# Batches 0 and 1 of the second norm, their transposes and their routing scores move into attention 2's last slots and drain; the scores move to another bank

## The reference

```python
x = x + layernorm(attention_1(layernorm(x)))          # 16 heads of 16, causal
x = x + layernorm(ffn(layernorm(x)))

# ffn(hidden):
h = rmsnorm(hidden, ln1_w)
q, k, v = h @ Wq, h @ Wk, h @ Wv                      # 32 query heads, 4 key/value heads, 128 wide
q, k = rope(q), rope(k)
o = softmax(causal(q @ k.T / sqrt(128))) @ v @ Wo     # attention 2
x = hidden + o
t = rmsnorm(x, ln2_w)
scores = sigmoid(t @ Wr)                              # 32 experts
idx = top_k(scores + expert_bias, 8)
w = scores[idx] / sum(scores[idx])
moe = sum over e of w_e * (silu(t @ Wg_e) * (t @ Wu_e)) @ Wd_e
return x + moe + silu(t @ Wsg) * (t @ Wsu) @ Wsd      # plus the shared expert
```

## Time and profile before

| | |
|---|---|
| median of 3 executions | 948.99 us (947.24 to 949.40) |
| the profiled execution | 950.87 us, of which the span from first to last instruction is 948.80 us |
| granted clock of PE, mean | 0.970 of full speed |
| PE busy | 867.5 us, 91% |
| DVE, ACT, POOL busy | 616.5 us (65%), 570.5 us (60%), 455.9 us (48%) |
| attention 2, slots 56 to 70 | from about 574 us to 651.3 us |
| block of the experts | from 651.76 us on |

### The profile page before, as it was taken

How to read it: one execution, slowest core, us unless ns; L and a number is a source line. 1 busy time by engine, 2 the same in 40 slices (tenths; PEclk the granted TensorE clock), 3 DMA queues, 4 the chain that set the end, 5 groups by cost and what they waited for, 6 DMA issues and landing times. The chain is left out here.

```text
span 948.8 us, 18792 instructions
## 1 busy us (share of the span) xinstructions
PE 867.5 (91%) x6108; PEld 802.1 (85%) x6108; DVE 616.5 (65%) x1620; ACT 570.5 (60%) x1570; POOL 455.9 (48%) x486
## 2 busy tenths in 40 slices
PE   5799998767999999999999999978999999999994
PEld 4699897657999998999899999867888888888884
DVE  5456667647787787778777777755444544544546
ACT  6788888656766766667666667654333333433333
POOL 3743334357867766777776777720222222221221
PEclk9799999978999999999999999997999999999998
DMA  7001000131114111421111111200433333333321
GB/s 234 1 1 46 22 23 1 59 93 39 35 46 142 38 45 35 114 66 46 34 46 35 46 45 36 51 1 18 144 116 116 114 98 115 101 114 116 112 82 45
DMA packets 50246, 63.34 MB, mean 67 GB/s; under 512 B 5728, under 2 KB 36064, under 8 KB 50176
## 3 DMA queue, kind: packets, MB, share of 16 engines
q1 hardware_dynamic: 49088, 61.41, 22.2%
q10 hardware_dynamic: 1088, 1.05, 0.3%
HBM read 41.86 MB, written 1.18 MB: 45 GB/s over the span
## 5 line engine op out<-in xcount | busy, mean ns | idle before, releaser
L639 POOL TENSOR_TENSOR b_prob<-b_prob,b_rsum 128x256 f32<-128x256 f32 (+1 forms) x128 | 104.7, 839 | 108.3 <-DVE b_rsum L621 108.3
L73 PE MATMUL banks<-act_t,b_w 128*128 128x256 f32 (+1 forms) x392 | 129.3, 330 | 3.9 <-DVE b_work L1194 2.8
L74 PE MATMUL banks<-act_t,b_w 128*128 128x256 f32 (+1 forms) x392 | 127.2, 324 | 0.0
L75 PE MATMUL banks<-act_t,b_w 128*128 128x256 f32 (+1 forms) x392 | 127.0, 324 | 0.0
L1955 ACT ACTIVATE moe_hid<-banks 128x512 fp32r<-128x512 f32 x66 | 39.5, 598 | 124.1 <-DVE banks L2046 124.1
L1355 ACT ACTIVATE b_prob<-banks,b_negmax 128x128 f32<-128x128 f32 (+1 forms) x256 | 103.6, 416 | 13.3 <-DVE b_negmax L1342 12.9
L2039 DVE TENSOR_TENSOR moe_gated<-banks,moe_share 128x512 f32<-128x512 f32 x66 | 45.6, 691 | 85.0 <-PE banks L75 80.9
L1211 ACT ACTIVATE b_qt<-b_work 128x512 fp32r<-128x512 f32 x64 | 40.5, 632 | 97.5 <-POOL b_work L1206 97.5
L639 POOL TENSOR_TENSOR a_prob<-a_prob,a_rsum 128x256 f32<-128x256 f32 x64 | 52.0, 834 | 82.2 <-DVE a_rsum L621 82.2
L1206 POOL TENSOR_TENSOR b_work<-b_work 128x512 f32<-128x512 f32 x64 | 86.7, 1355 | 9.2
L1202 POOL TENSOR_TENSOR b_work<-b_work,rope_t 128x512 f32<-128x512 f32 x64 | 84.2, 1315 | 8.2 <-DMA b_work<-b_work 8.2
(11 more groups left out here) (237 smaller groups left out, 3026.0 us busy)
## 6 DMA issues: line engine op xcount, KB each, us to landing
b_work<-b_work SPq DMA_DIRECT2D x128, 128.0 KB, 2.3
moe_share<-gates SPq DMA_DIRECT2D x32, 512.0 KB, 3.6
b_w_raw<-in_b_wq SPq DMA_DIRECT2D x4, 1024.0 KB, 5.5
b_w_raw<-in_b_wo SPq DMA_DIRECT2D x4, 1024.0 KB, 9.6
a_src_t<-act_t SPq DMA_DIRECT2D x5, 512.0 KB, 2.9
moe_w_raw<-in_wg SPq DMA_DIRECT2D x16, 128.0 KB, 2.2
moe_w_raw<-in_wu SPq DMA_DIRECT2D x16, 128.0 KB, 2.3
moe_w_raw<-in_wd SPq DMA_DIRECT2D x16, 128.0 KB, 2.3
```

Of the source, the lines that this page charges most:

```text
L73: nc.tensor.matmul(out, w_lo, m_hi, start=start, stop=False, skip_group_check=skip)
L74: nc.tensor.matmul(out, w_hi, m_lo, start=False, stop=False, skip_group_check=skip)
L75: return nc.tensor.matmul(out, w_hi, m_hi, start=False, stop=stop, skip_group_check=skip)
L639: last = self.m.nc.gpsimd.tensor_tensor(rows, rows, rsum[:, :, t:t + 1].to_broadcast([PART, 2, width]), ALU.mult)
```

## The change

The plans of PE, ACT and DVE in attention 2 are rewritten. Moments of batches 0 and 1 move from slot 64 to slots 56 and 60; their roots from slot 65 to slot 61, among the exps of slots 61, 62 and 63; their factors from 66 to 62; their rows from 67 to 63 and 64; their transposes from 68 to 63 and 64; their routing from 68 and 69 to 66 and 67. Batch 2's moments stay in slot 65, its roots go from 65 to 66, its rows stay in 67, its transposes in 68, its routing goes from 70 to 69. Batch 3's transposes go from slot 69 to 70. The banks of the transposes are permuted, so that batches 0 and 1 use the banks 4 and 5 that attention 2 frees first, and the routing scores go from bank 3, which holds transposed probabilities, to bank 4. Waits for the freed tiles are added. In the experts PE no longer waits for the sigmoid, since the sigmoid now reads another bank than the second gate product writes.

```diff
-        self.turn2 = Turn(m, ctx, "h2", rows, m.act_t, banks=(0, 1, 4, 5), weight=m.lnw[:, 1, :])
+        self.turn2 = Turn(m, ctx, "h2", rows, m.act_t, banks=(4, 5, 0, 1), weight=m.lnw[:, 1, :])
...
             def turn_h2(b):
-                pe.wait_ge(*{0: (self.exp_done, 2 * self.STAGES),
-                             1: (self.exp_done, 2 * self.STAGES),
-                             2: (self.kt_ready, self.ITS),
-                             3: (self.raw_ready, self.STAGES)}[b])
+                if b == 0:
+                    pe.wait_ge(self.kt_ready, self.ITS)
+                elif b == 1:
+                    pe.wait_ge(self.raw_ready, self.STAGES)
+                    pe.wait_ge(self.cos_ready, self.STAGES)
+                else:
+                    pe.wait_ge(self.exp_done, 2 * self.STAGES)
                 self.turn2.tensor(pe, b)
 
             def route(b):
-                pe.wait_ge(self.pt_ready, self.STAGES)
                 pe.wait_ge(self.turn2.lo_done, b + 1)
                 router_scores(m, b)
...
-                4: ((turn_h2, 0), (turn_h2, 1), (turn_h2, 2), (route, 0)),
-                5: ((turn_h2, 3), (route, 1)), 6: ((route, 2),)})
+                -1: ((turn_h2, 0),), 0: ((turn_h2, 1),), 2: ((route, 0),), 3: ((route, 1),),
+                4: ((turn_h2, 2),), 5: ((route, 2),), 6: ((turn_h2, 3),)})
...
             def rows(b):
+
+                if b == 0:
+                    for swapped in self.swapped:
+                        act.wait_ge(swapped, self.SWAPPED * (self.STAGES // 2))
+                elif b == 2:
+                    act.wait_ge(self.q_added, self.STAGES)
...
-                1: ((roots, 0), (roots, 1), (roots, 2), (expert_0, 0)),
-                3: ((rows, 0), (rows, 1), (rows, 2)),
-                4: ((turn, 0), (turn, 1), (roots, 3)), 5: ((rows, 3), (turn, 2)), 6: ((turn, 3),)})
+                -3: ((roots, 0), (roots, 1)), -1: ((rows, 0),), 0: ((rows, 1), (turn, 0)),
+                1: ((turn, 1), (expert_0, 0)), 2: ((roots, 2),), 3: ((rows, 2),), 4: ((turn, 2), (roots, 3)),
+                5: ((rows, 3),), 6: ((turn, 3),)})
...
-                0: ((moments, 0), (moments, 1)), 1: ((moments, 2),),
-                2: ((factors, 0), (factors, 1), (factors, 2)), 4: ((moments, 3), (turn, 0)),
-                5: ((factors, 3), (turn, 1)), 6: ((turn, 2), (turn, 3))})
+                -8: ((moments, 0),), -4: ((moments, 1),), -2: ((factors, 0), (factors, 1)), 0: ((turn, 0),),
+                1: ((turn, 1), (moments, 2)), 2: ((factors, 2),), 4: ((moments, 3), (turn, 2)),
+                5: ((factors, 3),), 6: ((turn, 3),)})
...
-        out = m.banks[:, 3, (NTT * b + t) * NE:(NTT * b + t + 1) * NE]
+        out = m.banks[:, 4, (NTT * b + t) * NE:(NTT * b + t + 1) * NE]
...
             pe_up(pe, 0, 0, 0)
-            pe.wait_ge(sigmoid_done, 1)
...
-            nc.scalar.activation(score[:].rearrange("p t e -> p (t e)"), gu[1][1][:, 0:NT * NE],
+            nc.scalar.activation(score[:].rearrange("p t e -> p (t e)"), m.banks[:, 4, 0:NT * NE],
```

## The result

| | median | range | runs |
|---|---|---|---|
| before | 947.79 us | 945.25 to 951.51 | 20 |
| changed | 950.91 us | 948.03 to 953.41 | 20 |

The ratio is 1.0031, 95% interval 1.0021 to 1.0040: slower by 2 to 4 us (3.1 between the medians), against 0.9 forecast. The profiled execution took 950.99 us (span 949.1).

A forecast was written before the change was run, and what follows sets the result against it. PE bounds the kernel, so the change acts only where PE waits, from slot 57 until the expert loop is full. +3.7 in front and -2.8 in the tail give +0.9: 949.9 us; 8-in-10 range 946.9 to 952.6.

The forecast's parts named there:

- slower: Outcome in which the time lies more than 0.2%, 1.9 us, above the kernel before; chance 0.27.
- What would show it: Signs listed: later marks in slots 60, 61; wait 2.7 us before slot 63; last projection 642.2; block 651.5 to 652.9.
- (a): Slot 57: batch 0's moments before the maximum delay POOL's chain; PE's slot 60 starts +0.86 us later, ends 0 to 1.28.
- (b): Slot 61: batch 1's moments before the maximum delay the reciprocal POOL waits for, with no slack: +1.28 us.
- (c): Slots 61 and 62: the roots' Sqrt load is hidden, but the Exp reload delays slot 62's exp: +1.28 us.
- (d): Drain, slots 63 on: factors and rows delay projection 59 by +0.8 us; the drain gives back 0.5.
- a rival: Slower by the clock: half clock in slot 63 after a longer wait, up to 1.5 us on projection 59; chance 0.28.
- (e): Tail behind the last projection: 2.8 us shorter at half clock, 4.0 at full clock; half clock was taken.
- The rival's total: Slower by the clock, with half clock in slot 63: together +2.4 us, 951.4; chance 0.28.
- (f): Things said to cost nothing: scores' bank, removed sigmoid wait, added waits, shared expert's weights; no DMA added or moved.
- the last part of the rival: First expert products: the clock rises later, gates find PE late, up to 1 us more, 952.3; chance 0.28.
- the intended gain: Rival: nothing in front is delayed, the tail's 2.8 to 4.0 us are gained, 945.0 to 946.2; chance 0.04.

The follow-up runs named there:

- the first two experiments: Kernel before with moments of batches 0 and 1 in slots 56 and 60: 951.18 us; the same with their roots in slot 61: 954.46 us.
- roots early: Kernel before with moments of batches 0 and 1 in slots 56 and 60 and their roots in slot 61: 954.46 us, ratio 1.0058.
- The fastest kernel: Changed kernel with moments of batches 0 and 1 before DVE's outputs of slots 62 and 63, their roots in slot 64, among other moves: 944.25 us, ratio 0.9958.

## Why the prediction was right in its range and wrong in its middle

The mechanism stood as forecast: a delay in front, a shorter tail, a difference small against both. The range held the time and the forecast of 949.9 was 1.0 us off, but the difference of 2 to 4 us is "slower" by the 1.9 us that I had set as the border, and I had given that 0.27. Part of the nearness is luck: I built on the 948.99 us of three executions, and over 20 the kernel before has 947.79. The difference, 3.1 us at the medians and 2.15 anchored, was missed by 2.2 and 1.25. The marks of "What would show it" that are times of the axis flatter the forecast in the same way: the last projection at 642.74 and the block at 652.15 lie near or within what I gave (642.2; 651.5 to 652.9), but this execution reached the anchor 1.82 us earlier than that of before. The sum by its steps, anchored:

| step | forecast | measured |
|---|---|---|
| (a) moments of batch 0 | +0.86 | +1.33 |
| (b) moments of batch 1 | +1.28 | +1.42 |
| (c) reload of the exp table | +1.28 | +1.42 (1.40 between the first two experiments, 1.37 without the loads) |
| (d) slot 63, clock kept | +0.8 | +0.96 |
| (d) rest of the drain | -0.5 | -0.2 |
| clock in slot 63 | 0 (a rival: +1.5) | +1.1 to +1.2 |
| (e) tail | -2.8 | -3.91 |
| first expert products | 0 | -0.06 |
| sum | +0.9 | +2.15 |

**(a) was mis-sized by how I used a wait.** I let POOL's 0.91 us in slot 58 absorb part of the 1.28. The wait shrank by 0.20, and POOL still started 1.32 late there, after 1.43 in slot 57. The wait names the reciprocal, which follows VectorE's query, ScalarE's query, and POOL's rotation of the slot before. In the changed kernel each of them waits for the next:

```profile
588.14 0.63 ACT L1211 ACTIVATE b_qt<-b_work 128x512 fp32r<-128x512 f32 x1 [2.58 <-POOL b_work L1206]
588.80 0.86 DVE L1216 TENSOR_TENSOR b_qt<-b_work,b_qt 128x512 fp32r<-128x512 f32 x1 [1.07 <-ACT b_qt L1211]
```

POOL was waiting for its own work to come round. The keys' transposes did come 0.86 later, as forecast (16.51 against 15.65), but the scores behind them waited for a split of the keys that ScalarE issues behind the exps, and those were a full 1.3 late. (b) and (c) went as written, 0.14 over each, which is mostly overlap lost: the first instruction of the moments begins 0.71 behind the addition where the maximum began 0.60 behind it, and the load of the table begins when the query has ended (614.78), where in the kernel before the exp began 0.09 ahead of the query's end.

**The clock in slot 63 is the step that failed.** Of two like cases in the profile of before, one with a fall and one without, I took none. I put the fall at nothing. It fell in both traces of the changed kernel and cost 1.1 to 1.2 us. The length of the wait does not decide it: it fell behind a wait of 1.18 and stayed behind one of 1.19, and of the waits of 2.61 it fell behind two and stayed behind one. What decides there is open; I can only say that with the wait filled it stayed up, in one trace. The rival's total, 951.4, was nearest to the result.

**(e) erred the other way.** I chose half clock for batch 2's routing. It ran at 2.4 GHz (1.00 in 647 to 648), so the tail was shorter by 3.91 and not 2.8, close to the 4.0 that I had worked out for full clock. Both numbers compare with a tail of before at half clock. The old order at nearly full clock took 10.71 instead of 13.32 (roots early), so 2.6 of the 3.91 depend on where the clock falls, and only 1.3 are left between 10.71 and 9.41. The two wrong choices of clock nearly cancel, +1.15 and -1.1, which is luck. What is left, +1.2, is (a) to (d), each under-estimated by 0.1 to 0.5.

(f) held, with one addition: the gates stand ready 1.82 later and PE comes 0.9 behind them, since the clock rose 4.8 us into the expert products instead of 2.9. That is the last part of the rival, but up to the first common wait it cost nothing (-0.06), not up to 1. Without that fall the gates' wait of 1.36 us is back and 1.3 us are saved, most of it in the block's 12 products, which ran at half clock before as well.

The fastest kernel answers the question where the intended gain went: with the clock fallen, the shorter tail is worth over 4 us, and the changed kernel paid for it by three insertions in a loop of engines (4.2 us) of which none had to be there. Between 1 and 1.5 us of the 3.1 between the medians are not in this account.

## What to carry to other kernels

An engine's idle time can hide work only if what ended it doesn't depend on the engine where the work goes: follow the releaser back one round, and a wait that leads back to the same engine is a cycle, in which an insertion costs its full length. Move a stage that switches ScalarE's table behind the last use of the table that it evicts; the price is the reload on the chain, not the load that you see. Where the clock may fall, forecast both cases as sums of their own, and compare kernels from a common instruction ahead of the change, not by their spans.

## What the runs showed of the hardware that was not expected

- The reload costs its 1.28 us and hardly more: the exp starts at 616.08, where the load that began at 614.78 ends at 616.06, and removing it gave 1.37 on the chain. By "ScalarE: Activation LUTs", section "What ACT_TABLE_LOAD costs", of the Trainium skill another 1380 ns of drain would come with it; the five loads of the changed kernel from slot 61 on show none (0.01 to 0.02 us to the next activation).
- The fall of the clock doesn't follow the length of the wait before slot 63 (0.85 us: stayed; 1.18: fell; 1.19: stayed; 2.59: fell; 2.61: stayed once, fell twice), and once it came with PE busy 1.00 in each of the five microseconds before it (638 to 643, fill in the fastest kernel's tail). From the anchor it came at the same place within 1.2 us in the two executions of either kernel.
- A VectorE operation on 128 x 2 elements took 0.16 us alone, and 0.81 (L155) beside POOL's normalising, which it shared no data with; the same in slots 63 and 64 (0.82 for L155, 0.89 for L173). Each ended within 0.03 us of POOL's operation, while L145 and the reciprocal L170 kept their lengths beside it.
